# Attention's idle buffers and banks lent to the first and the last tile group of a mixture-of-experts block, with ACT beginning part of the transfers

## The reference

```
x = x + 0.5 * ffn(layernorm(x))
x = x + attention(layernorm(x))
x = x + 0.5 * ffn(layernorm(x))          # the same ffn weights

ffn(f):    shared = sum over 2 shared experts of (silu(f@wg_s) * (f@wu_s)) @ wd_s       (width 128)
           probs  = softmax(f @ router_w), 16 experts; the top 2, their weights made to sum to 1
           routed = sum over the 2 chosen experts of weight * ((silu(f@wg_r) * (f@wu_r)) @ wd_r)  (width 64)
attention: 16 heads of 16, q k v with biases; scores * 0.25 + a one-sided linear (ALiBi) bias,
           the first 8 heads looking back and the last 8 forward; softmax; @ v; @ Wf + bf
```

## Time and profile before

| | |
|---|---|
| Median of three runs | 2431.34 us |
| The profiled execution | 2442.57 us |
| Its span, first to last instruction | 2440.8 us |
| PE busy | 1838.3 us (75%) |
| DVE busy | 1411.0 us (58%) |
| ACT busy | 1017.9 us (42%) |
| POOL busy | 940.8 us (39%) |
| Mean granted clock of PE | 0.845 |

### The profile page before, as it was taken

How to read it: one execution, slowest core, us unless ns; L and a number is a source line. 1 busy time by engine, 2 the same in 40 slices (tenths; PEclk the granted TensorE clock), 3 DMA queues, 4 the chain that set the end, 5 groups by cost and what they waited for, 6 DMA issues and landing times.

```text
span 2440.8 us, 34106 instructions
## 1 busy us (share of the span) xinstructions
PE 1838.3 (75%) x10516; PEld 1217.7 (50%) x10516; DVE 1411.0 (58%) x3675; ACT 1017.9 (42%) x2015; POOL 940.8 (39%) x999
## 2 busy tenths in 40 slices
PE   4568885577889888878779777876888898845770
PEld 3455664354656565545445444544655565523550
DVE  5454445657655555567678777775565655563332
ACT  2224442244444444535445444543454554521330
POOL 3432325643432322153554455444233221254416
PEclk8777897888979898978899889988898998976685
DMA  6346663634775566644463546358475656449875
GB/s 181 110 139 210 186 211 125 132 87 96 215 189 150 159 160 176 151 129 86 94 135 88 89 106 134 84 94 257 126 184 142 190 148 155 142 128 300 269 256 155
DMA packets 313027, 376.46 MB, mean 154 GB/s; under 512 B 39304, under 2 KB 256008, under 8 KB 312840
## 3 DMA queue, kind: packets, MB, share of 16 engines
q1 hardware_dynamic: 276880, 289.84, 45.6%
q0 software_dynamic: 24576, 67.14, 10.0%
q10 hardware_dynamic: 11392, 17.31, 2.3%
HBM read 180.71 MB, written 146.80 MB: 134 GB/s over the span
## 4 chain that ended last, share of the span: by engine, by line
PE 45%; DVE 14%; DMA 13%; issue 9%; SPq 8%; another core or an unknown queue 4%; POOL 4%; ACT 2%; ACTq 0%; POOLq 0%; DVEq 0%
PE bank L986 7%; DMA den<-o_store 6%; PE bank L977 6%; PE bank L870 4%; PE bank L1080 4%; PE bank L872 4%; PE bank L871 4%; PE bank L1060 4%; PE bank L1027 3%; PE bank L1093 3%; PE bank L967 2%; SPq L818 2%; DVE den L1525 2%; DVE row_max L1428 2%
## 5 line engine op out<-in xcount | busy, mean ns | idle before, releaser
L1428 DVE TENSOR_REDUCE row_max<-bank 128x1 f32<-128x512 f32 (+2 forms) x768 | 349.2, 504 | 188.9 <-PE bank L1043 121.9
L1206 ACT ACTIVATE p_buf<-bank 128x512 f32<-128x512 f32 x640 | 361.3, 596 | 223.9 <-PE bank L1060 134.0
L1639 POOL TENSOR_SCALAR_AFFINE_SELECT p_buf<-p_buf 128x512 f32<-128x512 f32 x256 | 160.8, 642 | 420.8 <-ACT p_buf L1206 420.1
L1027 PE MATMUL bank<-k_stack,q_stack 99*128 99x512 bf16 (+3 forms) x1024 | 258.5, 323 | 78.3 <-issue 48.9
L1583 POOL DMA_INDIRECT sorted_x<-xn,position x256 | 250.4, 978 | 107.3 <-issue 69.5
L1060 PE MATMUL bank<-q_stack,k_stack 101*128 101x512 bf16 (+3 forms) x1024 | 244.6, 316 | 62.3 <-issue 18.3
L1605 POOL DMA_INDIRECT y_tok<-sorted_y,position x216 | 206.4, 956 | 192.0 <-DVE x_ffn L1495 65.1
L986 PE MATMUL bank<-t_w,t_h 64*128 64x256 f32 x752 | 244.4, 451 | 41.9 <-DVE t_h L1482 30.4
L977 PE MATMUL bank<-t_xt,t_w 128*128 128x256 f32 x752 | 237.3, 444 | 48.1 <-DMA t_w<-expert_w 32.6
L1080 PE MATMUL bank<-p_buf,v_rows 128*32 128x512 f32 (+3 forms) x2048 | 197.6, 488 | 15.0 <-POOL p_buf L1639 10.4
L986 PEld LDWEIGHTS bank<-t_w,t_h 64*128 64x128 f32 x752 | 142.7, 210 | 118.7 <-DVE t_h L1482 50.6
(11 more groups left out here) (165 smaller groups left out, 3591.4 us busy)
## 6 DMA issues: line engine op xcount, KB each, us to landing
t_w<-expert_w SPq DMA_DIRECT2D x188, 256.0 KB
t_x<-sorted_x SPq DMA_DIRECT2D x188, 256.0 KB
sorted_y<-t_y SPq DMA_DIRECT2D x188, 256.0 KB
q_stack<-qk_part SPq DMA_DIRECT2D x192, 128.0 KB
k_stack<-qk_part SPq DMA_DIRECT2D x192, 128.0 KB
sorted_x<-zeros SPq DMA_DIRECT2D x68, 256.0 KB, 3.6
o_store<-o_raw ACTq DMA_DIRECT2D x64, 256.0 KB
x_ffn<-in_L_attn_x SPq DMA_DIRECT2D x16, 512.0 KB, 4.9
```

The source lines that it names most:

```text
L1027: pe.matmul(ps[:, col:col + k1 - k0], q_stack[0:ROWS_S, h, P * qt:P * qt + P], k_stack[0:ROWS_S, h, k0:k1], start=(n == 0), stop=False, sk ...
L1206: act.activation(p_of(u), psum("score", *of)[:, :], ACT.Exp).then_inc(*exp_done.step(*of))
L1428: ins = dve.tensor_reduce(row_max[g % 2][:, n:n + 1], src[:, col:col + q1 - q0], X, ALU.max)
```

## The change

`GROUPS` becomes 12 and 4 sequences in layer 1, so the tiles are 39, 55, 63 and 31 (188 as before). The groups (0, 0) and (1, 1) are marked as `many_tiles`. For these:

- Four tile inputs and six tile weights lie in `p_buf`, in place of three and three buffers of their own; SP waits until attention no longer uses it (or, at the start, until attention's raw weights, which moved from `y_tok` to `p_buf`, are converted).
- Their pieces may hold six banks (`wide`) in place of three.
- ACT issues half of the zero fills and every transfer of a tile's result.

For layer 0, the sequences 2 to 5 have input and norm buffers of their own in `q_stack` and `k_stack`, so that their loads no longer wait for a put, and a third buffer of transposed activations lies in `y_tok`. The constant rows of the stacks are loaded after that use. For layer 1, the gathers go round five buffers, `y_tok` and the four in the stacks, for both groups; so those of the first group (but for `y_tok`) also wait for the end of attention.

For all 188 tiles, the output product is split over two halves of PE's rows: DVE writes the hidden values of tokens 128 to 255 on partitions 64 to 127 (one product of 256 columns becomes two of 128), the two products write two banks, and ACT copies them by two instructions of 256 columns. The planner's assumed durations are changed with it (PE 1.1 to 0.65, DVE 0.84 to 0.98, ACT 0.6 to 0.8, a fill 13 to 20.8 or twice 10.4 side by side), and the gathers' table lookup is put earlier.

```diff
-GROUPS = (((0, 6), (6, 16)), ((0, 11), (11, 16)))
+GROUPS = (((0, 6), (6, 16)), ((0, 12), (12, 16)))
...
-BANKS = {"row": 3, "score": 2, "out": 1, "fill": 3}
+BANKS = {"row": 3, "score": 2, "out": 1, "fill": 3, "wide": 6}
+EARLY = range(2, min(6, GROUPS[0][0][1]))
+def many_tiles(l, g):
+    return (l, g) in (ALL_GROUPS[0], ALL_GROUPS[-1])
+def first_buffer(b):
+    return b if b in EARLY else b % 2
...
 def norm_buffer(kind, l, b):
-    return 1 if kind == "att" else b % 2 if l == 0 else 0
+    return 1 if kind == "att" else first_buffer(b) if l == 0 else 0
...
 def y_buffer(l, b):
-    return 1 + (b - LAST) % 4 if l == 1 and b >= LAST else 0
+    return b % 5 if l == 1 else 0
...
+    def fill(kind, l, b):
+        return "wide" if kind == "ffn" and (l == 0 and b < GROUPS[0][0][1] or l == 1 and b == B - 1) else "fill"
...
+        part(at - 2.5, "SP", 0.8, x, *fills, *sent, *last,
+             takes=[("wide_x" if many_tiles(l, g) else "t_x", ("t_x", l, g, j), [(flip, "PE")])], lag=4.5)
+        part(at - (4.0 if many_tiles(l, g) else 2.5), "SP", 0.9, weights, (("table", l, g), "DVE"),
+             (("expert weights",), "SP"), *last,
+             takes=[("wide_w" if many_tiles(l, g) else "t_w", ("t_w", l, g, j), [(made, "PE")])], lag=4.5)
...
-        part(at + 1.0 * pace, "PE", 1.1, made, (hidden, "DVE"), takes=[
-            bank("fill", ("ty", l, g, j), (made, "ACT"))], lag=0.3)
+        part(at + 1.0 * pace, "PE", 0.65, made, (hidden, "DVE"), takes=[
+            bank(fill, ("ty", l, g, j, t), (made, "ACT")) for t in range(2)], lag=0.3)
...
+            if not many_tiles(1, g):
+                at = max(at, start + 16 * (B + 1) + 12.6 + 0.1 * b)
             gathering(at, 1, b)
...
-        t_x = [sb(f"t_x{i}", [P, 2, D]) for i in range(3)]
-        t_w = [sb(f"t_w{i}", [P, ND * P + D]) for i in range(3)]
+        t_x = [sb(f"t_x{i}", [P, 2, D]) for i in range(3)] + [
+            p_buf[0][:, i, :].rearrange("p (t d) -> p t d", d=D) for i in range(4)]
+        t_w = [sb(f"t_w{i}", [P, ND * P + D]) for i in range(3)] + [p_buf[c][:, i, :] for c, n in ((1, 4), (2, 2))
+                                                                     for i in range(n)]
...
+        for flat, of in ((q_flat, x_ffn), (k_flat, xn)):
+            of += [flat.bitcast(F32)[:, NT * D * i:NT * D * (i + 1)].rearrange("p (t d) -> p t d", d=D)
+                   for i in range(4)]
...
-                    for e in range(E):
+                    for e in range(0, E, 2 if many_tiles(l, g) else 1):
...
                 elif name == "tile out":
                     l, g, j = of
-                    pe.wait_ge(*th_step.at(*of, "u"))
-                    ps = take(("ty", *of), ty_out, *of)
+                    pe.wait_ge(*th_step.at(*of, "u", 1))
+                    halves = [take(("ty", *of, t), ty_out, *of, t) for t in range(2)]
                     for t in range(2):
-                        ins = pe.matmul(ps[:, D * t:D * t + D], hidden[:, P * t:P * t + P],
-                                        weights[0:ME, ND * P:ND * P + D], start=(t == 0), stop=(t == 1),
-                                        skip_group_check=True)
+                        at = slice(ME * t, ME * t + ME)
+                        ins = pe.matmul(halves[t][:, 0:D], hidden[at, :], weights[at, ND * P:ND * P + D],
+                                        start=True, stop=True)
...
+                elif name == "fill":
+                    for e in range(1, E, 2):
+                        row = act.value_load(fill_i[0:1, e:e + 1])
+                        act.dma_start(sorted_x[l, g][bass.ds(row, RT), :].rearrange("(i p) d -> p i d", p=P),
+                                      zeros[:, :].unsqueeze(1).broadcast_to((P, 2, D))
+                                      ).then_inc(*filled_act.step(l, g, e))
...
-                    act.activation(t_y[i][:, :, :].rearrange("p t d -> p (t d)"), psum("ty", *of)[:, :],
-                                   ACT.Copy).then_inc(*ty_out.step(*of))
+                    for t in range(2):
+                        act.activation(t_y[i][:, t, :], psum("ty", *of, t)[:, 0:D], ACT.Copy
+                                       ).then_inc(*ty_out.step(*of, t))
+                    if many_tiles(l, g):
+                        act.wait_ge(*ty_out.at(*of, 1))
+                        act.dma_start(put_rows(*of), t_y[i][:, :, :]).then_inc(*ty_put_act[i].step(*of))
...
-                    dve.tensor_tensor(t_h[i][:, :], ps[ME:P, 0:RT], t_h[i][:, :], ALU.mult
-                                      ).then_inc(*th_step.step(*of, "u"))
+                    for t in range(2):
+                        at = slice(P * t, P * t + P)
+                        dve.tensor_tensor(t_h[i][ME * t:ME * t + ME, :], ps[ME:P, at], t_g[:, at], ALU.mult
+                                          ).then_inc(*th_step.step(*of, "u", t))
```

More of the change, by code:

```diff
@@ L266, in transposes @@
             piece = "transpose", kind, l, b, d
-            takes = [bank("fill", ("xt", kind, l, b, d), (piece, "DVE"))]
+            takes = [bank(fill(kind, l, b), ("xt", kind, l, b, d), (piece, "DVE"))]
             if d == 0:
@@ L308, in shared @@
             part(at[4 + half], "PE", 1.65, down, *[(("split", l, b, j), "POOL") for j in range(NSH)],
[L309 removed]
+                 takes=[bank(fill("ffn", l, b), ("y", l, b, half), (down, "DVE"))], lag=0.3)
             part(at[4 + half], "DVE", 0.69, down, (down, "PE"))
@@ L317, in tile @@
         sent = [(("position", l, b), "POOL") for b in range(*GROUPS[l][g])]
-        part(at - 2.5, "SP", 0.8, x, (("fill", l, g), "SP"), *sent,
-             takes=[("t_x", ("t_x", l, g, j), [(flip, "PE")])], lag=4.0)
-        part(at - 2.5, "SP", 0.9, weights, (("table", l, g), "DVE"), (("expert weights",), "SP"),
-             takes=[("t_w", ("t_w", l, g, j), [(made, "PE")])], lag=4.0)
+        fills = [(("fill", l, g), "SP")] + ([(("fill", l, g), "ACT")] if many_tiles(l, g) else [])
+        last = [(("values", B - 1, NG - 1, 2), "PE")] if (l, g) == ALL_GROUPS[-1] else \
+            [(("attention weights",), "DVE")] if (l, g) == ALL_GROUPS[0] else []
@@ L332, in tile @@
-        part(at + 1.0 * pace, "ACT", 0.6, made, (made, "PE"),
-             takes=[("t_y", ("t_y", l, g, j), [(put, "SP landed")])])
-        part(at + 2.0 * pace, "SP", 0.57, put, (made, "ACT"), lag=3.0)
+            bank(fill, ("tgu", l, g, j), (hidden, "DVE")), ("t_h", ("t_h", l, g, j), [(made, "PE")])], lag=0.3)
+        part(at + 0.6 * pace, "ACT", 0.38, hidden, (hidden, "PE"),
+             takes=[("t_th", ("t_th", l, g, j), [(hidden, "DVE")])])
+        part(at + 0.6 * pace, "DVE", 0.98, hidden, (hidden, "ACT"))
@@ L336, in gathering @@
     def gathering(at, l, b):
         g = group_of(l, b)
-        made = [(("tile put", l, g, j), "SP") for j in range(n_tiles(l, g))]
+        made = [(("tile out", l, g, j), "ACT landed") if many_tiles(l, g) else (("tile put", l, g, j), "SP landed")
+                for j in range(n_tiles(l, g))]
         gather, combine = ("gather", l, b), ("combine", l, b)
-        part(at, "DVE", 1.15, gather, (("table", l, g), "DVE"), (("position", l, b), "POOL"), *made)
+        part(at - 1.0, "DVE", 1.15, gather, (("table", l, g), "DVE"), (("position", l, b), "POOL landed"))
```

175 lines of the change are left out of this document (112 added, 63 removed).

## The result

The changed kernel takes 2306.43 us, the median of four runs (2289.72 to 2310.03), beside 2425.81 us for four runs of the kernel before on the same chip (2410.47 to 2434.01): a ratio of 0.950, 95% interval 0.944 to 0.956, or 119 us less. The forecast was 2341, the range 2262 to 2405.

A forecast was written before the change was run, and what follows sets the result against it. No one bound: the start waits for buffers, the middle is near PE's limit, the tail near the DMA engines' limit, ending in POOL's issue. Terms -25, -2, -3, -20, -6, -8, -26 sum to -90 from 2431.3: 2341 us, range 2262 to 2405.

The forecast's parts named there:

- rival 1: PE packs well and the start becomes full: the product's 0.53 us a tile counts, 2276 us in all; chance 0.17.
- First sequences: Layer 0, 60 to 160 us: own buffers for sequences 2 to 5 end the loads' wait; -25 us, bounds 0 to -40.
- Fills: Zero fills at the start and in the tail: the DMA engines limit them, so ACT's half gives -2 and -3 us.
- The product: Output product of every tile: two row halves side by side save 0 to 0.53 us a tile, taken 0.3.
- The four weight loads do not shrink: Output product of each tile: its weight loads of 0.21 us, 0.84 together, gain nothing from the row halves.
- Tiles of (0, 0): 39 tiles, 188 to 392 us: more banks and buffers and the split product; -20 us, bounds 0 to -39.
- Tiles of (0, 1) and attention: Middle, 616 to 1124 us and attention with 63 tiles on four sequences: -6 and -8 us.
- The sequences without tiles: Attention in the middle: sequences with no tiles beside them stay at about 82 us each.
- The tail: From 2222 us on: faster stream of tiles and gathers, four last sequences in place of five; -26 us, bounds -10 and -40.
- Rival 3: The long group's tiles run past attention's end, some eleven of them, and delay gathers: +37 us, 2378; chance 0.10.
- the stream at 2.75 us a tile plus 7.5 a sequence: Tail: tiles and gathers share the DMA engines at 286 GB/s; 136 us in place of 157, -21.
- Rival 4: Middle: 118 tiles each needing two of three `fill` banks stall PE, 0.9 us a tile, +106; 2461 us; chance 0.10.

The follow-up runs named there:

- e5: Changed kernel without the early loads: sequences 2 to 5 share two buffers again, as in the kernel before; 2321.83 us, ratio 0.953.
- e4: Changed kernel with SP again issuing every zero fill and every store of a tile, none from ACT; 2315.31 us, ratio 0.951.
- e1: Changed kernel with both output products of a tile on PE's rows 0 to 63, so they can't run side by side; 2325.91 us, ratio 0.959.
- e10: Kernel before with the changed kernel's planner durations alone: new written order, same instructions; 2403.17 us, ratio 0.986.
- e2: Kernel before with the packed output product alone (two banks, split DVE and ACT steps, planner durations for these); 2362.97 us, ratio 0.976.
- e6: Changed kernel with the `wide` limit at three banks in place of six; 2340.43 us, ratio 0.962.
- e7: Changed kernel with three buffers for tile inputs and three for weights in first and last group, not four and six; 2322.21 us, ratio 0.954.
- e3: Changed kernel with groups of 11 and 5 sequences in layer 1 again, in place of 12 and 4; 2298.81 us, ratio 0.951.
- e8: Changed kernel with the 63 tiles of layer 1's first group paced at 0.8 of a unit each, not 1.0; 2297.63 us, ratio 0.950.
- e11: Changed kernel with one gather buffer for layer 1's first-group sequences and four for the last group's, as before; 2337.47 us, ratio 0.960.
- e9: Changed kernel with all gathers of layer 1 made to wait until the last group's last tile is put away; 2333.30 us, ratio 0.958.

## Why the prediction was right, and which terms were not

The direction and the range held (2306 in 2262 to 2405). The measured time lies about as near to rival 1 (2276) as to the forecast (2341), but not by rival 1's mechanism, as the product's term below shows. The sum of -90 was made of terms of which several are off, most of them too small; measured is -119 by the medians and -153 by the profiles. The terms below are from the profiles, so together they are some 34 us too large.

- **First sequences**: forecast -25, measured -15.5 to SP's first fill and -18.2 to `fill_i`. The mechanism is the forecast one, e5 shows that it is all of it. PE did work at a higher share (0.71 of 60 to 148, 0.59 before), not at the 0.87 I had used as the limit, and DVE is now as full (0.72).
- **Fills**: -2 and -3 forecast, -0.6 and -4.3 measured (27.5 to 26.9 and 30.1 to 25.8 us from `fill_i` to the first tile). The sum fits, the reasoning only in part: from SP alone the same kernel would need 34.6 and 31.7 (e4). The change made SP begin its fill later, which the prediction did not see, and ACT's half makes up for it. (Its sum 17.1 / 16 x 3 is 3.2, not 3.3; nothing hangs on it.)
- **The product**: 0.53 us a tile was the upper bound, and PE's busy time fell by just that. "The four weight loads do not shrink" was wrong: their busy time fell by more than half. What reached the end was 0.12 us a tile by e1's ratio (23 us over 188 tiles) and 0.13 by that of e10 to e2, under half of the 0.3 that I took; single stages of the profiles show 0.24 to 0.35. PE was not the only thing that tiles waited for.
- **Tiles of (0, 0)**: -20 forecast, -36 measured from first tile to last. e6 gives the banks 16 of them, e7 the buffers 3, e1 the product about 11 (179 us without it). But part of it may be work moved behind the stage, as e6 suggests.
- **Tiles of (0, 1) and attention**: -6 and -8 forecast, -49 and -40 measured in the profiles, both outside the stated bounds (-29 and -27 at the far end). This is the term that failed. I held the written order to be neutral and priced only instructions. The planner's new durations alone bring 32 us in the stage of 55 tiles and 19 in that of group (1, 0) (e10), while the six sequences without tiles take 11 longer and the tail 12; over the whole kernel it is 34. Packing adds 15 in the stage of group (1, 0) (e1). The sequences without tiles were forecast rightly: 82.5 us for 81.7. That 63 tiles could cost less than 59 did follow from PE's side of my estimate (-27), and I had leaned to the other.
- **The tail**: -29 forecast with its fill, -2 measured. Rival 3's condition came true here: the long group ran past attention's end, with eight tiles and not eleven, and the first gathers came 73 us later than before, relative to the projection of sequence 15. Its price of 37 us did not show: without the run-over the kernel takes as long (e3, e8). Five buffers are worth 28 us (e11). The step that was wrong in kind is the stream at 2.75 us a tile plus 7.5 a sequence at the DMA engines' rate. The engines were not the limit while POOL issued: a tile alone costs 2.3, a sequence's gathers 10.3, and they nearly add up. 31 x 2.3 + 16 x 10.3 = 236, and from the first tile to the end it took 229.

So the total is near the forecast by luck: a large gain that I had not seen, the order's, stood against a tail gain that did not come. That the order's 34 us of e10 carry over whole into the changed kernel is not shown; e1's stage of 55 tiles says so for that stage alone.

Rival 4's stall cost nothing in the middle: e2 ran in three `fill` banks and gained 59 us. In the first and last group three banks in place of six do cost, 16 and 22 us of tile stage (e6). The Trainium skill warns that row tiles write to different banks and so need more of them ("TensorEngine Tiling (Array Packing)", Gotcha 1: PSUM Pressure). The traces agree in the stages dense with tiles and show no price in the middle.

## What to carry to other kernels

Where a program orders the instructions from assumed durations, a change of these durations is an edit of its own: run the old instructions in the new order too. Here that brought some 34 us without a changed instruction, though one of the new durations was false for them, and it would otherwise be booked to the packed product. Before overlapping two streams, run them one after the other once: if the end hardly moves, there was little overlap, and an edit that only shifts the stall will not pay. Work that saves PE time counts by the chain around it; here about a quarter of it reached the end.

## What the hardware showed that was not expected

- While POOL issued gathers of 128 rows back to back, one each 1.25 us, PE hardly advanced after the first 8 us: 4.9 us of work in 48, its signals some 11 us apart, at a DMA share of 0.48. With runs of 8 gathers and pauses the same tiles went through in 108 us, without gathers in 71. That they nearly take turns is shown by e9 and e11; why is not. The records of PE lie well ahead of its signals there, so the profile does not say what PE waits for, and nothing was run that separates issue, the tables of rows, or the memories involved.
- Products of 64 rows by 128 with 256 columns in float32 pair on the two row halves: 1.13 us for four becomes 0.70, and the weight loads pair too (142.7 to 62.1 us busy over 188 tiles). Two banks alone do not do it: 1.13 us in e1.
- Half of a 16-transfer fill on a second issuer raises the DMA share from 0.80 to 0.96 and brings the first tile 7.7 us forward, some 4.5 of them because ACT begins while SP waits.
